# Loading the picked rows after the last used tile, and forming the recurrence biases after the row sums

## The reference, cut to what matters

```python
# h: (16, 126, 128)
xf = layernorm(h).reshape(2016, 128)
tw = routing_weights(xf, Wr, br, Wgate, bgate)   # 2 of 4 groups, 2 of 4 experts in each
out = 0
for e in range(16):
    out = out + tw[:, e:e + 1] * ((silu(xf @ W1[e]) * (xf @ W3[e])) @ W2[e])
h = h + out
x = layernorm(h)
gx = x @ Wx0 + b0          # then Wx1, b1 for the second layer
# per step: g = gx_t + h @ Wh; gates; c_new = f * c + i * c_tilde; h_new = o * tanh(c_new) + m_new
```

## Time and profile before

| what | value |
|---|---|
| time, three runs | 974.0, 975.0, 978.17 us; median 975.0 |
| time of the profiled execution | 974.72 us |
| its span | 972.9 us |
| TensorE busy | 827.9 us (85%) |
| VectorE busy | 737.6 us (76%) |
| ScalarE busy | 499.1 us (51%) |
| GpSimd busy | 364.6 us (37%) |
| mean granted TensorE clock | 0.898 of full |

### The profile page before, as it was taken

How to read it: one execution, slowest core, us unless ns; L and a number is a source line. 1 busy time by engine, 2 the same in 40 slices (tenths; PEclk the granted TensorE clock), 3 DMA queues, 4 the chain that set the end, 5 groups by cost and what they waited for, 6 DMA issues and landing times.

```text
span 972.9 us, 44506 instructions
## 1 busy us (share of the span) xinstructions
PE 827.9 (85%) x17239; PEld 673.0 (69%) x17239; DVE 737.6 (76%) x3032; ACT 499.1 (51%) x1605; POOL 364.6 (37%) x565
## 2 busy tenths in 40 slices
PE   4567877833999999994799999999999999998595
PEld 2246655522666666662489999999999999985253
DVE  4347798599786776776689999999999999977144
ACT  0535676820765565552445555555555555555083
POOL 0315574657677777772001111111111111100653
PEclk9776897855999999997779999999999999999697
DMA  7710000620122222224500000000000000002133
GB/s 237 279 63 1 1 1 16 217 67 17 39 74 80 77 80 79 77 53 120 165 5 1 0 0 0 0 0 0 0 0 0 0 0 0 0 3 67 46 100 116
DMA packets 30138, 50.64 MB, mean 52 GB/s; under 512 B 7970, under 2 KB 19162, under 8 KB 30075
## 3 DMA queue, kind: packets, MB, share of 16 engines
q1 hardware_dynamic: 23578, 36.95, 12.2%
q0 software_dynamic: 6496, 12.84, 4.9%
HBM read 38.40 MB, written 11.38 MB: 51 GB/s over the span
## 4 chain that ended last, share of the span: by engine, by line
PE 41%; DVE 4%; POOL 4%; DMA 3%; issue 2%; ACT 1%; SPq 0%; POOLq 0%; DVEq 0%
PE quad L1469 11%; PE quad L1476 9%; PE bank L1469 9%; PE bank L1476 8%; POOL y_scratch L1806 2%; DMA post<-y_scratch 2%; POOL x_scratch L1800 2%; PE bank L1496 1%; PE quad L1496 1%; DVE post L1663 1%; DVE post L1928 0%; PE bank L1453 0%; DVE post L1318 0%; DVE stream L2084 0%; SPq L870 0%
## 5 line engine op out<-in xcount | busy, mean ns | idle before, releaser
L1469 PE MATMUL quad<-post,area 128*128 128x32 f16 (+1 forms) x3760 | 176.4, 182 | 0.0
L1476 PE MATMUL quad<-post,area 128*128 128x16 f16 (+1 forms) x3760 | 175.1, 172 | 1.4 <-DVE post L1702 0.9
L1476 PEld LDWEIGHTS quad<-post,area 128*128 128x128 f16 x3760 | 144.8, 96 | 4.6 <-DVE post L1702 3.2
L1418 POOL COPY post<-post 128x32 f32 (+1 forms) x126 | 27.1, 215 | 309.5 <-DVE post L1709 309.5
L1476 PE MATMUL bank<-post,area 128*128 128x16 f16 (+1 forms) x3130 | 135.1, 171 | 4.6 <-DVE post L1702 2.4
L1469 PE MATMUL bank<-post,area 128*128 128x32 f16 (+1 forms) x3130 | 138.5, 181 | 0.2 <-issue 0.2
L1469 PEld LDWEIGHTS quad<-post,area 128*128 128x128 f16 x3760 | 137.6, 96 | 0.0
L1611 ACT ACTIVATE post<-post 128x32 f32<-128x32 f32 x252 | 57.8, 230 | 132.3 <-DVE post L1677 132.3
L1476 PEld LDWEIGHTS bank<-post,area 128*128 128x128 f16 x3130 | 110.8, 96 | 6.2 <-DVE post L1702 3.0
L1469 PEld LDWEIGHTS bank<-post,area 128*128 128x128 f16 x3130 | 106.5, 96 | 0.3 <-issue 0.3
L1663 DVE TENSOR_REDUCE post<-bank 128x48 f32<-128x96 f32 x378 | 88.8, 262 | 13.9 <-PE bank L1469 2.5
(11 more groups left out here) (337 smaller groups left out, 1939.2 us busy)
## 6 DMA issues: line engine op xcount, KB each, us to landing
w0s<-in_w SPq DMA_DIRECT2D x12, 768.0 KB
area<-in_rec SPq DMA_DIRECT2D x7, 640.0 KB
post<-y_scratch SPq DMA_DIRECT2D x8, 504.0 KB
area<-in_w SPq DMA_DIRECT2D x4, 768.0 KB
area<-in_f SPq DMA_DIRECT2D x2, 1024.0 KB, 7.7
area<-in_patches SPq DMA_DIRECT2D x1, 1488.4 KB
x_scratch<-post SPq DMA_DIRECT2D x1, 1472.0 KB, 7.3
area<-in_taps SPq DMA_DIRECT2D x1, 1350.0 KB
```

What stands on the lines that cost most here:

```text
L1469: mm = pe.matmul(chunk_at(l, q, m, first, operand.shape[1]), rec_w[:, w, 0, m * P:(m + 1) * P], operand, start=False, stop=False, skip_gro ...
L1476: mm = pe.matmul(chunk_at(l, q, m, first, operand.shape[1])[:, :, 0, :], rec_w[:, w, 1, m * P:(m + 1) * P], operand[:, :, 0, :], start=Fal ...
```

## The change

A count of the used tiles is already formed in the routing: the running sum over the experts, at expert 15. Three small VectorE instructions behind `dst_row` make from it, for each of the four write semaphores, the count that stands for the used tiles alone, 16 x ceil((used - u) / 4) for u = 0 to 3. SP loads these four integers into registers and waits for them in place of the constants, so the loads of the picked rows are issued when the last used tile's rows are out. The waits for all 78 tiles move to `rec_sp`, behind the wait for the finished row sums and ahead of the loads for the last part. On VectorE, only `centre` stays ahead of the mixing, and the rest of `biases` moves behind the last `add_rows`. Eight words are added to the scratch layout, so that what lies behind them moves by 32 bytes.

```diff
--- before.py
+++ after.py
@@ -68,6 +68,7 @@
 PICKS = 4
 PAIRS = PICKS * TOKENS
 NT = (PAIRS + E0 * (P - 1)) // P
+FILLED = (PAIRS + P - 1) // P
 COMBOS = PICKS * TILES
 XW2 = 2 * D
 XG, LOOK = 7, 5
@@ -225,6 +226,8 @@
         dst_row = view(NT).bitcast(I32)
         expert_f = view(2, SEQ)
         expert_at = view(NT, 1).bitcast(I32)
+        rounds_f = view(YR, 1)
+        rounds_at = view(YR, 1).bitcast(I32)
         PAIR_AT = at[0]
 
 
@@ -814,8 +817,9 @@
         LATE_USED = (PICKS * TOKENS // 2 + P - 1) // P
 
         AFTER = {"taken": 1, "logit_shift": 2, "expert_f": 3, "place": 4, "expert_at": 5, "src_row": 6, "dst_row": 7,
+                 "rounds": 8,
                  "logits": 1, "prefix": 2, "expert_ps": 3, "table": 4,
-                 "taken1": 8, "slot": 9, "expert1_f": 10, "expert1": 11, "prefix1": 5, "expert1_ps": 6}
+                 "taken1": 9, "slot": 10, "expert1_f": 11, "expert1": 12, "prefix1": 5, "expert1_ps": 6}
 
         IF = 2 * RH
         REC_PARTS = ((slice(0, IF), W_SCALE / 2), (slice(IF, GP), W_SCALE))
@@ -835,6 +839,10 @@
             if g < EARLY:
                 return f"fetched{g}", 16 * (W_FETCHES[g] + 1)
             return ("x_out", 16 * (NBLK + 1)) if g == EARLY else ("rec_in", 16 * (7 + 1))
+
+        def rounds_of(sp, u):
+            return sp.value_load(rounds_at[0:1, u:u + 1], min_val=16 * ((FILLED - u + YR - 1) // YR),
+                                 max_val=16 * ((NT - u + YR - 1) // YR))
 
         def ffn_sp(sp):
             for e in range(EARLY, E0):
@@ -863,8 +871,10 @@
                     sp.wait_ge(sg("rec_low"), w)
                 sp.dma_start(rec_raw, rec_in[w]).then_inc(sg("rec_in"), 16)
 
+            sp.wait_ge(sg("route_dve"), AFTER["rounds"])
+            rounds = [rounds_of(sp, u) for u in range(YR)]
             for u in range(YR):
-                sp.wait_ge(sg(f"y_out{u}"), 16 * ((NT - u + YR - 1) // YR))
+                sp.wait_ge(sg(f"y_out{u}"), rounds[u])
             for g in range(TILES // 2):
                 rows = g * 2 * SEQ * PICKS
                 sp.dma_start(y_all[:, 2 * g:2 * g + 2],
@@ -1243,6 +1253,11 @@
             dve.scalar_tensor_tensor(out=dst_row, in0=row_f[:, 0:NT], scalar=-1.0, in1=src_f, op0=ALU.add, op1=ALU.add
                                      ).then_inc(sg("route_dve"), 1)
 
+            link(dve, dve.tensor_scalar(rounds_f, number(N_COUNT, YR, 1), tiles(4)[0:1, E0 - 1:E0], -1.0 / YR,
+                                        ALU.subtract, ALU.mult))
+            link(dve, dve.tensor_scalar(rounds_f, rounds_f, 0.5 - 0.5 / YR, WHOLE, ALU.add, ALU.add))
+            dve.tensor_scalar(rounds_at, rounds_f, WHOLE, 16.0, ALU.subtract, ALU.mult).then_inc(sg("route_dve"), 1)
+
             dve.tensor_reduce(top_p[:, 0, :], pick, AX, ALU.add)
             link(dve, dve.tensor_reduce(top_p[:, 1, :], second, AX, ALU.add))
             link(dve, dve.tensor_tensor(top_p[:, 2, :], top_p[:, 0, :], top_p[:, 1, :], ALU.add))
@@ -1304,7 +1319,7 @@
                                                        in1=rec_w[:, w, 0, part], op0=ALU.mult, op1=ALU.subtract)
                     ins.then_inc(sg("rec_low"), 1)
 
-            biases(dve)
+            dve.tensor_tensor(centre, ident, mean_mat[:, :], ALU.subtract).then_inc(sg("bias"), 1)
             for g in range(TILES // 2):
                 for k in range(1, PICKS):
                     for t in (2 * g, 2 * g + 1):
@@ -1324,13 +1339,13 @@
                     add_rows(dve, st_blocks[j], bank[MIX_BANK[j]][:, 0:BLK], j + 1)
             add_rows(dve, st_blocks[NBLK - 1][:, 0:HALF_BLK], bank[MIX_BANK[NBLK - 1]][:, 0:HALF_BLK], NBLK)
             add_rows(dve, st_blocks[NBLK - 1][:, HALF_BLK:BLK], bank[1][:, 0:HALF_BLK], NBLK + 1)
+            biases(dve)
 
         def add_rows(dve, rows, mix, ready):
             dve.wait_ge(sg("mixed_ps"), ready)
             dve.tensor_tensor(rows, rows, mix, ALU.add).then_inc(sg("routed"), 1)
 
         def biases(dve):
-            dve.tensor_tensor(centre, ident, mean_mat[:, :], ALU.subtract).then_inc(sg("bias"), 1)
             dve.wait_ge(sg("recb_in"), 16)
             for s in range(3):
                 link(dve, dve.tensor_copy(bias_cast[0:96, :, s, :], bias_raw[0:96]))
@@ -1381,6 +1396,8 @@
 
         def rec_sp(sp):
             sp.wait_ge(sg("routed"), NBLK + 1)
+            for u in range(YR):
+                sp.wait_ge(sg(f"y_out{u}"), 16 * ((NT - u + YR - 1) // YR))
             sp.dma_start(fc_w, fcw_in).then_inc(sg("fcw_in"), 16)
             sp.dma_start(b2_row, fb2_in.rearrange("(z e) d -> z e d", z=1)).then_inc(sg("fg_in"), 16)
             sp.dma_start(fg_w, fg_in).then_inc(sg("fg_in"), 16)
```

## The result

Six runs of the changed kernel have a median of 965.03 us (963.36 to 967.15), beside 974.5 us for six runs of the kernel before (971.48 to 978.76): a ratio of 0.9906, interval 0.988 to 0.9933. Forecast were 966.0 us and, against 975.0, a ratio of 0.991. The profiled execution took 966.81 us with a span of 965.0, against 974.72 and 972.9. Two later sets on other occasions gave 0.987 (0.9829 to 0.9912) and 0.9905 (0.9873 to 0.9938) for the same kernel.

The account below looks back on a forecast made before the run. The mixing was taken as bound by loads of picked rows that start late and then move at 224 GB/s. Terms: -10.6 + 1.2 + 0.2 + 0.2 = -9.0 us, so 966.0 us against the median 975.0; range 962 to 970.

Parts of the forecast that it names:

- The earlier start: Between tiles and recurrence, all eight loads of picked rows can be issued 10.6 us earlier, behind tile 71's write.
- What the loads collide with: Writes of tiles 73 to 77 among the early loads cost 1.2 us; delay of the writes themselves costed at 0.
- Rival B: Tile 73's write waits for the four loads issued ahead, holding `keep` of tile 77: 968.5 us, 7%.
- Mixing bound by VectorE or loads: In the mixing, loads set the gain, 10.6 us; VectorE's ceiling is 11.2 us, 0.6 us to spare.
- Biases moved: Behind the last `add_rows`, 3.11 us of biases in VectorE's 2.99 us hole delay the reciprocal by 0.2 us.
- Three small instructions: In the routing on VectorE, they take some 0.65 us and cost 0.2 us, between 0 and 0.4.
- Rival A: TensorE still at 1.2 GHz in the mixing's tail, about 3 us more: 969 us, 15%.
- Rivals C and D: C: tile 73's write waits behind all eight loads, 978 to 981 us, 4%; D: early start unused, 975 us, 4%.

Follow-up runs that it names:

- thirty instructions more: The changed kernel, four buffers, with 30 clearings of one spare word each added in VectorE's tile loop: 967.62 us, ratio 0.9917.
- the change plus two: The changed kernel, four buffers, with one VectorE clearing ahead of the routing split in three, so the recurrence's loop stands two instructions later: 963.1 us, ratio 0.9877.

## Why the prediction was right, and where not, step by step

**The earlier start** is right. SP issued the loads at 440.92, 6.9 us ahead of the last down matmul, and before 3.8 us behind it: 10.7 us, forecast 10.6. Tile 71's write had landed at 440.85, so the waits with register values did not hold the loads up.

**What the loads collide with** was mis-sized on the side of the writes; on the side of the loads it can't be told. I charged the loads 1.2 us for the writes among them. In the profile of the change the waits of ScalarE for loads end at 449.35, 451.70, 453.69 and 455.80, 2.15 us apart, while before they were 2.30 apart. Windows of the change:

```profile
446.00:450.00 4.00, 1.66 (x16) 1.15 (x16) 1.39 (x4) 3.13 (x7) 1.94 (x2) 1.00 0.92 269
450.00:454.00 4.00, 0.41 (x2) 0.36 (x2) 2.49 (x10) 1.05 (x5) 1.03 (x1) 0.80 0.93 289
```

Loads and writes together moved 269 to 289 GB/s. Since the loads' own rate differs between profiles by more than that, the 1.2 us can be neither confirmed nor refuted. Tile 73's write, which I costed at 0 against 5.6 us of room, landed after 8.8 us, 6.5 more than a write alone. **This is the step that failed**: "I cost this at 0". `keep` of tile 77 waited 4.04 us in the first profile, and 2.35 and 1.53 us in the later ones of the same kernel. I had taken the longest landing of the trace before, 4.8 us beside a single load, for the longest there could be beside eight. One of the prediction's own signs of being wrong, `keep` of tile 77 waiting for a write, was there each time.

**Rival B** is right in kind, and its number fits the first profile: it had `keep` of tile 77 at 451.8 and the last pair at 465.3; the profile has 451.51 and 464.84, in an execution that reached the last down matmul 0.9 us later. From last down matmul to last pair it is 17.1 us; the forecast had 15.7, rival B 18.4, and before it was 25.1. In the two later profiles of the same kernel it is 15.4 and 14.6 us, no worse than the forecast.

Its rule, that the write lands with the fourth load, is not what the traces show. When tile 73's write was issued in the first profile, three loads were out (440.92, 441.34, 442.24), and it landed 2.3 us ahead of the fourth load, for which ScalarE waited until 453.69. In the third profile one load was out, issued 0.04 us before the write, and the write still took 6.3 us. In the profile between them, with the first load issued 0.44 us ahead, it took 7.2 us, and with thirty instructions more, at 1.6 us ahead, 8.9 us. So even a write issued together with the first load lands late. More loads ahead of it cost more, but not in step: in the change plus two, with the first load 2.1 us ahead, it was 8.3 us. By what rule the write is held is not shown. The Trainium skill ("DMA: Bandwidth & Descriptors", Queues, rings and completion order) has a DMA engine alternate between queues by whole packets. The 6.5 us lie between the estimates from its typical packet (2.5) and from its ceiling (9.3); the typical one, by which I had let the sum stand, does not cover them if the write waits for one packet only. No run shows the packets themselves.

**Mixing bound by VectorE or loads.** I had VectorE and the loads in step within 0.6 us, and took the loads as the bound. With VectorE held for 4 us it was VectorE, and with 1.53 us it was still VectorE, whose additions ran without a gap there too. That the median came out within 1 us of the forecast all the same was in part luck, for two reasons that I had not in the sum: the wait was shorter in other executions, and the recurrence was a little faster (1853 to 1859 matmuls per 50 us in the first profile of the change, 1845 to 1852 before), worth 1.2 us there. The second is not the mixing's doing, by the windows above.

**Biases moved**: right. The reciprocal started at 470.97, and the root on ScalarE ended at 470.82, so with the 0.11 us that lay between the two before, the biases cost some 0.04 us, forecast 0.2. Their worth with early loads is 2.9 us, forecast 3.1.

**Three small instructions**: forecast 0.2 us. They took 0.52 us (237.49 to 238.01), and from the first turn to the last down matmul the profile of before has 208.6 us and that of the change 208.6. Any cost is below what differs between executions.

**Rival A, the clock**: partly. The end of the mixing found TensorE at 1.2 GHz:

```profile
462.00:466.00 4.00, 4.00 (x13) 1.54 (x12) 4.00 (x15) 1.65 (x4) 0.00 (x0) 0.50 0.00 0
466.00:470.00 4.00, 3.92 (x18) 1.93 (x17) 3.21 (x11) 2.14 (x4) 0.00 (x0) 0.99 0.12 37
```

It came back at about 466, ahead of the last centring, so it cost only the squares, transposes and centring ahead of that. From the last pair's start to the reciprocal it was 5.6 us before and 6.1 in the change, 5.6 and 6.7 in its repetitions: 0 to 1.1 us, not 3. Rivals C and D did not occur.

## What to carry to other kernels

When a transfer is started earlier, look at what else will be in the DMA queues by then, and ask who needs those transfers to land: a small write that took 2.3 us alone took 6.3 to 8.9 beside eight loads of 504 KB, and an engine that executes in order waited for it although its own data were ready. Size such a wait with room for a multiple of what the quiet trace shows. Two more buffers took the wait away here, but no total showed a gain from them. And where one half of a change only pays through the other (here the moved work that late loads used to hide), test each alone: the biases alone were worth nothing, and behind early loads they were worth 2.9 us of the stretch.

## What the runs showed that I had not expected

The same eight loads of one program ran at 224 GB/s in one execution and, in a kernel that differs from it only behind the tiles, at 291 to 311 GB/s in another, with the DMA engines 91 to 92% busy in both. Each of these two kernels has one profile, and what sets the rate is not shown. An argument that rests on the rate in a single profile carries that spread: 0.65 us for each load, 5 us over eight.

The recurrence, which is bound by TensorE at full clock, ran 1% slower (1826 to 1835 matmuls per 50 us instead of 1841 to 1859) in two profiles of one kernel on two chips. The same kernel with two more clearing instructions on VectorE, some 280 us ahead of the recurrence, did not have it, on a third chip. This is some 4 us, close to half of the whole change, beside an edit that does no work; its cause is open.
